# VectorE in place of GpSimd for the low parts of the gated tiles, in the last two chunks of the first feed-forward

## The reference

```
xn = layernorm(x)
x  = x + linear_attention(xn) + ffn0(xn)      # block 0
xn = layernorm(x)
x  = x + softmax_attention(xn) + ffn1(xn)     # block 1

ffn0(x):   up = x @ wu.T;  gate = x @ wg.T    # ternary weights, 1024 wide
           hidden = silu(up) * gate
           return hidden @ wd.T               # ternary weights
```

## Time and profile before

| | |
|---|---|
| median of 3 runs | 741.36 us (740.01 to 742.01) |
| profiled execution, its time | 741.94 us |
| its span, first to last instruction | 740.0 us |
| PE busy | 696.3 us (94%) |
| DVE busy | 524.2 us (71%) |
| ACT busy | 438.6 us (59%) |
| POOL busy | 295.8 us (40%) |
| mean granted TensorE clock | 0.975 |

### The profile page before, as it was taken

The page is one execution under the profiler, slowest core; times in us unless marked ns, Lnnn a source line. Parts: engine busy times, 40 slices in busy tenths (PEclk is TensorE's granted clock), DMA queues, the critical chain, the costliest instruction groups (busy, mean ns, idle before and its releaser), DMA issues.

```text
span 740.0 us, 10943 instructions
## 1 busy us (share of the span) xinstructions
PE 696.3 (94%) x4186; PEld 437.3 (59%) x4186; DVE 524.2 (71%) x856; ACT 438.6 (59%) x600; POOL 295.8 (40%) x269
## 2 busy tenths in 40 slices
PE   3788899989999899999999998999999999999998
PEld 3576798977787778677677673333333333333345
DVE  4877866555578366678788878888897288888315
ACT  2454334446544532432432336999998899999883
POOL 1118846347657843542543431122224223333410
PEclk7799999999999999999999998999999999999999
DMA  6127101003024553423110112244444244423321
GB/s 260 57 77 279 58 0 58 1 2 115 0 86 152 182 166 98 140 90 115 57 58 2 57 58 76 80 144 151 139 138 149 93 147 141 157 90 94 102 81 58
DMA packets 25847, 74.13 MB, mean 100 GB/s; under 512 B 4620, under 2 KB 5996, under 8 KB 24964
## 3 DMA queue, kind: packets, MB, share of 16 engines
q1 hardware_dynamic: 21268, 65.37, 26.4%
q0 software_dynamic: 3808, 7.60, 3.5%
q10 hardware_dynamic: 720, 0.48, 0.2%
HBM read 54.54 MB, written 23.06 MB: 105 GB/s over the span
## 4 chain that ended last, share of the span: by engine, by line
PE 62%; POOL 2%; DVE 2%; ACT 1%; issue 1%; DMA 1%; SPq 0%; DVEq 0%; POOLq 0%; ACTq 0%
PE PS L1029 17%; PE PS L767 12%; PE PS L1015 12%; PE PS L773 9%; PE PS L998 6%; PE PS L988 5%; DVE mx L1329 1%; POOL sg L1642 1%; ACT P L1541 1%; DMA scr_k<-spl 1%; POOL rot L1663 1%; POOL rot L1662 1%; PE PS L1004 0%; ACT spl L1523 0%; ACT us L1506 0%
## 5 line engine op out<-in xcount | busy, mean ns | idle before, releaser
L1541 ACT ACTIVATE P<-PS 128x1024 f32<-128x1024 f32 x256 | 249.2, 1023 | 31.9 <-PE PS L1015 31.6
L1336 DVE TENSOR_REDUCE mx<-PS 128x1 f32<-128x512 f32 x300 | 189.2, 683 | 34.3 <-PE PS L998 32.7
L1329 DVE TENSOR_REDUCE mx<-PS 128x2 f32<-128x1024 f32 x106 | 124.8, 1221 | 37.4 <-PE PS L988 37.0
L1029 PE MATMUL PS<-P,VV 128*32 128x512 f32 x1024 | 137.6, 609 | 0.1
L1633 POOL TENSOR_TENSOR hl<-sg,hh 128x512 fp32r<-128x512 f32 x64 | 85.2, 1332 | 116.7 <-ACT hh L1511 67.4
L1015 PEld LDWEIGHTS PS<-QS,KS 64*128 64x128 f32 x512 | 48.9, 185 | 124.3 <-ACT P L1541 111.2
L1015 PE MATMUL PS<-QS,KS 64*128 64x512 f32 x512 | 117.7, 459 | 2.3 <-DVE mx L1329 1.8
L998 PE MATMUL PS<-KM,QM 64*128 64x512 f32 x300 | 82.0, 401 | 0.0
L1497 ACT ACTIVATE sg<-PS,cols 128x512 f32<-128x512 f32 x32 | 22.0, 688 | 82.1 <-PE PS L767 82.1
L1642 POOL TENSOR_TENSOR sg<-sg,us 128x512 f32<-128x512 f32 x32 | 42.1, 1316 | 37.5 <-ACT us L1506 37.5
L767 PE MATMUL PS<-XH,UGH 128*128 128x512 f32 x128 | 54.2, 423 | 1.6 <-ACT sg L1497 0.8
(11 more groups left out here) (211 smaller groups left out, 1346.6 us busy)
## 6 DMA issues: line engine op xcount, KB each, us to landing
QM<-scr_q SPq DMA_DIRECT2D x16, 512.0 KB, 4.4
KM<-scr_k SPq DMA_DIRECT2D x16, 512.0 KB, 5.3
QS<-scr_q SPq DMA_DIRECT2D x16, 512.0 KB, 4.3
KS<-scr_k SPq DMA_DIRECT2D x16, 512.0 KB, 5.2
scr_q<-spl SPq DMA_DIRECT2D x24, 256.0 KB, 3.3
scr_k<-spl SPq DMA_DIRECT2D x24, 256.0 KB, 3.4
scr_o<-OE POOLq DMA_DIRECT2D x14, 256.0 KB, 2.7
stg<-in_tern SPq DMA_DIRECT2D x3, 1024.0 KB, 4.8
```

Source lines behind the costliest of these rows:

```text
L1029: i = e.matmul(PS[32 * c:32 * c + 32, 7, :], v_head(8 * b + kt, 2 * j + c // 2), P[s % 4][:, chunk(c // 2 + 2 * (c % 2))], start=(kt == 0) ...
L1329: e.tensor_reduce(mx[p % 2][:, :, qt, half], PS[:, b:b + 2, :], AX.X, ALU.max).then_inc(q["mx"], 2)
L1336: e.tensor_reduce(mx[p % 2][:, h, qt, half:half + 1], bank[b], AX.X, ALU.max).then_inc(q["mx"], 1)
L1541: e.activation(P[s % 4][:, half * 1024:(half + 1) * 1024], PS[:, b:b + 2, :].rearrange("p b n -> p (b n)"), ACT.Exp).then_inc(q["ex"], 1)
```

## The change

In chunks 2 and 3 (c >= WHOLE) of layer 0, POOL's part of `up` no longer makes the low part. A new piece `low_part` is put into the list instead, which only DVE takes: the low part of tile m-1 right behind the `up` of tile m, and that of tile 7 behind the down of tile 5. What is computed is the same. Chunks 0 and 1 and layer 1 keep POOL.

```diff
             yield from part("up", layer, c, m, pf.next())
+            if not layer and c >= WHOLE and m:
+                put("low_part", c, m - 1)
             yield
...
         for m in (5, 6, 7):
             yield from part("down", layer, c, m)
-            if layer and m == 5:
-                put("hidden", c, 7)
+            if m == 5 and (layer or c >= WHOLE):
+                put("hidden" if layer else "low_part", c, 7)
             yield
...
+            def low_part(c, m):                      # on VectorE
+                f = 8 * c + m
+                e.wait_ge(q["hh"], f + 1)
+                e.tensor_tensor(hl[f % 4][:, :], sg[f % 3][:, :], r32(hh[f % 4][:, :]), ALU.subtract).then_inc(q["hl"], 1)
...
             def up(layer, c, m, b):                  # on GpSimd
                 f = 32 * layer + 8 * c + m
-                if layer == 0:
+                if layer == 0 and c < WHOLE:
                     low_part(f)
-                else:
+                elif layer:
```

More of the change, by code:

```diff
@@ L1389, in last @@
                         e.tensor_tensor(xs, bank[acc[2 * cc + i]], xs, ALU.add).then_inc(q["ly"], 1)
-            parts = {f.__name__: f for f in (start, ln_stats, ln_norm, ln_turn, bias, w0l, signs, tern_scale, tern_cut, spread_vb, add_vb, half, scales, kv_in, kv_sums, q0,
+            parts = {f.__name__: f for f in (start, low_part, ln_stats, ln_norm, ln_turn, bias, w0l, signs, tern_scale, tern_cut, spread_vb, add_vb, half, scales, kv_in, kv_sums, q0,
                                              kv_sum, att_n, att_t, att_b, gate, up, ffn_end, prep_down, prep_ug, qk, qk_split, max_half, max_join, recip, join, project, last)}
```

## The result

The changed kernel takes 744.46 us (median of 6 runs, 742.94 to 745.72), the kernel before 741.34 us beside it: ratio 1.0041, 95% interval 1.0026 to 1.0055. The medians are 3.1 us apart, and the interval is 1.9 to 4.1 us slower. The forecast was 743.8 in a range of 741.2 to 746.2, slower as the likelier side.

The account below looks back on a forecast made before the run. PE was busy 94% of the span, so a change was taken to count only where PE waits. Terms 0.2 + 2.05 + 0.15 gave +2.4 us on a median of 741.36, so 743.8 us, range 741.2 to 746.2.

Parts of the forecast that it names:

- Turns between the two engines: A DVE operation with two SBUF inputs issued inside a POOL operation waits for its end; POOL's next waits for DVE.
- Place 1: Chunk 2's layernorm: tile 1's low part stands ahead of `ln_norm` and delays ACT's normalisation; +0.2 us (bounds 0 and 0.7).
- Place 2: End of chunk 2: tile 7's low part is held inside POOL's last total, PE waits at down 7; +2.05 us.
- Place 3: Chunk 3's layernorm: low parts of tiles 2 and 3 delay `ln_stats`, POOL's power and `nmr`; PE +0.6 us for the moment.
- Place 4: End of chunk 3: last stall moves from POOL to DVE, equally long, PE +0.45; +0.15 us together with Place 3.
- A: End of chunk 2: no collision around 186 us, tile 7's low part slips through; 741.8 us, chance 0.17.
- B: End of chunk 3: relieved POOL pays, no collision at 186 and the 1.55 us wait goes; 740.1 us, chance 0.11.
- C: Clock falls behind the new 2 us PE wait at 186.6, costing 1.7 us more; 745.5 us, chance 0.18.
- D: End of chunk 3: last low part loses its turn to `qk_join`, 1.25 us more on PE; 745.0 us, chance 0.09.

Follow-up runs that it names:

- e1: Changed kernel, but POOL's second total waits until DVE has made the low part of chunk 2's tile 7; ratio 1.0000 to the kernel before.
- e7: Changed kernel, but the low part of chunk 2's tile 7 subtracts a PSUM bank instead of `hh` (output not the reference's); ratio 1.0016 to the kernel before.
- e5: Changed kernel, collision included, but POOL's first `qk_join` waits until DVE has written `nmr` of chunk 3's layernorm; ratio 1.0039 to the kernel before.
- e3: Kernel before with only chunk 3's low parts moved to DVE, chunk 2's staying on POOL; ratio 1.0006 to the kernel before.
- e8: Only chunk 3's low parts on DVE, those of tiles 2, 3 and 7 placed anew, first `qk_join` waiting for `nmr`; ratio 0.9973 to the kernel before.
- e9: Changed kernel with the waits of e1 and e5 and chunk 3's tiles 2, 3 and 7 placed as in e8; ratio 0.9966 to the kernel before.
- e10: Only chunk 3's low parts on DVE, tile 7's placed behind the down of tile 4; ratio 0.9997 to the kernel before.

## Why the prediction was right, and where it was off

**What bounds the kernel.** Right. The change added 8.6 us to DVE's busy time and took 19.5 from POOL's, and what moved the time was PE's own waits. A low part that nothing holds takes 0.68 us, a little more than the 0.64 I took from `spl`.

**Turns between the two engines.** Right, in both directions: e1 and e7 show it by taking away either side. The last GpSimd difference was held as well, 2.71 us instead of 2.39 beside DVE's low part of tile 6.

**Place 1, the first layernorm, +0.2.** Right. From DVE's multiply before it (149.05 before, 148.33 after) to PE's first matmul behind it (161.21, 160.65) it is 12.16 and 12.32 us: +0.16. The way was right too: from the same multiply `nmr` starts 0.6 us later (7.07 and 7.68 us), ACT's normalisation 0.14 (7.73 and 7.87).

**Place 2, the end of chunk 2, +2.05.** Right: 9.38 - 7.31 = 2.07. The low part of tile 6 came first at the boundary (182.87, 0.69 us), and that of tile 7 met the last total 0.09 us after its start; the four profiles with the bare collision have PE's wait at 1.90 to 1.92 us.

**Place 3, the second layernorm, +0.6.** This is the term that was too small. The delay of the queue was right: from down 7 of chunk 2 to the second pair of transposes it is 24.93 us before and 25.62 in e5, +0.7. But with `nmr` held (e1) it is 26.62, +1.7. I sized `nmr` at its 0.16 us, though it has two SBUF inputs, like a low part, and did not ask what GpSimd would do at that moment without its own low part: it begins `qk_join`. My own rule of the turns said what follows; I applied it to the large instructions only. The price was even in the trace before, at the next layernorm:

```profile
239.49 1.29 POOL L1633 TENSOR_TENSOR hl<-sg,hh 128x512 fp32r<-128x512 f32 x1 [0.74 <-ACT hh L1511]
...
239.76 1.04 DVE L1132 SCALAR_TENSOR_TENSOR nmr<-mv,rstd 128x4 f32<-128x4 f32 x1
```

In chunk 3 the hold cost 0.9 us (74.36 in e1 against 73.46 in e5), and in six of eight profiles about 1.2 us of clock.

**Place 4, the end of chunk 3, -0.45 against place 3.** Right in kind: `spl` 1.30 instead of 2.77, the last wait moved from POOL to DVE, 0.92 to 1.27 us where I had as long as before (1.55). I put that wait at about 229.7; it came at 233.24, later by the hold of `nmr` and by the two low stretches of the clock ahead of it. With `nmr` free (e5) places 3 and 4 together come to 73.46 - 73.36 = +0.10 against the forecast +0.15; in the changed kernel without loss of clock (e1) they are +1.0.

**The sum.** Forecast 0.2 + 2.05 + 0.15 = 2.4. Measured parts: 0.16 + 2.07 + 1.0 = 3.2, and the clock at the layernorm, about 0.9 in the mean of the eight profiles. That is 4.1, at the upper end of what the runs allow (1.9 to 4.1) and 1 us over what was measured. The distances of e1 and e3 say more than their ratios too: e1 is +1.0 at `VV` and 0.0 (-0.9 to +0.9) over the whole, e3 +2.1 and +0.4 (-0.4 to +1.3). So about 1 us comes back behind `VV`, where the distances don't reach. One candidate is on record. Of the five profiles with `nmr` free, four had the clock low behind the wait for `VV`; of the eight with `nmr` held, two. From the end of that wait to the end of the span the five take 479.2 us in the mean and the eight 478.1. That this is the cause, and why the clock should fall less often there, isn't shown: single profiles scatter from 477.2 to 480.2. So it is in part luck that the sum came near. It left out 0.9 us of hold and about 0.9 of clock at the layernorm, and also the 1 us or so that came back.

**The rivals.** A (no collision) was what e1 and e7 made by hand: their ratios, 1.0000 and 1.0016, are 0 and +1.2 us, to either side of its +0.4. B (the relieved POOL pays) didn't happen by itself, but e8 and e9 show that the gain was there. It needed the place of tile 7 and a free `nmr` together; tile 7's place alone gave 0.9997 (e10). C (the clock behind the 1.9 us wait) came in one profile of four and cost 1.35 us there, not 1.7; more often the clock was lost at the layernorm, for which I had no term. D (the last low part loses its turn to `qk_join`) didn't happen: it took 0.68 us, and `qk_join` was held instead (1.66 us instead of 1.29). The chance of slower by over 0.3% should read 0.52 (0.25 + 0.18 + 0.09), not 0.51.

## What to carry to other kernels

Before elementwise work is moved from GpSimd to VectorE, list the VectorE instructions with two SBUF inputs near it, the tiny ones too, and lay GpSimd's long operations beside them: what counts is not the busy share of either engine but whether such an instruction falls into a GpSimd operation while TensorE waits for it. Where it does, a wait on the other side (GpSimd after VectorE) or a piece placed one step earlier costs little: the first took back nearly the whole loss here (e1), and both together turned 0.4% slower into 0.3% faster (e9). Removing work from an engine moves what stands behind it forward, possibly into the way of an instruction on the other engine that had just got through ahead of it, as `nmr` did.

## What was not expected of the hardware

- A 128x4 operation of 0.16 us was held until the GpSimd operation ended, like a large one: it took 1.24 us behind a GpSimd operation of 1.28 that began 0.06 us before it.
- A wait of 1.9 us on a busy TensorE cost clock in one of four profiles, while the layernorm, where TensorE waits 1.3 and 0.6 us with four small transposes between, cost it in six of eight.
